# Skip product of a state-space layer folded into the addition of its outputs on VectorE

## The chip, the cores and the metric

The program runs on one core of one Trainium2 chip. The metric is the device time of one execution in microseconds (us); the time before is a median of three runs. One execution was also recorded by the hardware profiler, and every row of a trace below comes from that one.

## What is computed

The reference is one layer: a state-space mixer (Mamba-2 style, 16 sequences of 512 tokens, model width 128, inner width 256 in 4 heads), a layer norm, a mixture of 8 experts with 2 per token, and a second layer norm. The part that the change is about is the last term of the scan's output:

```
def step(h, inp):
    dA_t, dt_t, x_t, B_t, C_t = inp
    dBx = (dt_t[:, :, None] * x_t)[..., None] * B_t[:, None, None, :]
    h = dA_t[:, :, None, None] * h + dBx
    y = jnp.einsum('bn,bhpn->bhp', C_t, h) + D[None, :, None] * x_t
    return (h, y)
...
yn = y * jax.lax.rsqrt(jnp.mean(y * y, axis=-1, keepdims=True) + EPS) * norm_w
y = yn * jax.nn.silu(z)
return y @ Wout.T
...
x = _layernorm(x + _L0_attn_ref(x, ...), axis=-1)
x = _layernorm(x + _L0_ffn_ref(x, ...), axis=-1)
```

`D[None, :, None] * x_t` is the skip product: the activated channels of x, each times one number of its head.

## The kernel before, in words

Everything is written out by hand for each engine, with semaphores between the engines; each engine takes its instructions strictly in the order of the program. There is no scheduler.

**Stages.** A prologue turns the inputs of all sequences and starts sequence 0. Then come 16 slots, one for each sequence. Slot s does three things at once: it scans sequence s (`scan`), it projects and convolves sequence s + 1 (`project`), and it normalises and routes sequence s - 1 (`route`). After the slots, 135 tiles of 128 sorted rows go through the experts, and the last sums and norms close the program. Slot 0 has no sequence to route but finishes the softplus of all others (lines 1345 to 1347); slot 15 has nothing to project.

**A slot.** A slot goes over four chunks of 128 tokens, c = 0 to 3. For each chunk:
- TensorE (`slot_pe`) turns x and B (lines 652, 654), takes the outer products of C with the state for c > 0 (L658), projects a block of the next sequence (L483), adds up the chunk's output in PSUM bank `p7` (L676, L682), and makes the new state in `p6` (L691).
- VectorE (`slot_dve`) makes `Xdt` (L1313), `carried` (L1319), the mask `M` of the following chunk (L1107) and three taps of the convolution (L1033) of the next sequence; then the output `yv` (L1335), which is `p7` plus the skip product `xD`; then the new state (L1340 for c = 0, L1343 after it). In chunk 0 the layer-norm statistics of the routed sequence (L1140, L1144, L1147) stand between `Xdt` and `M`.
- ScalarE (`slot_act`) copies B (`Btok`, L907), takes exponentials (L773), the convolution's first tap (L815) and the squares of the outputs (`square`, L868, of `yv` into `ysq`).
- GpSimd multiplies `yv` by the gate (`gate_y`, L1547) and decays states, and scatters rows.

After chunk 3 TensorE computes the first gate block (L491), the sums of squares (L712, which waits for all four squares), the output product (L720), the inner products of the next sequence (L580) and the second gate block (L491 again). ScalarE then loads the table for Silu and goes through `activate` (L821, four of 128x512 into `xc`), `skip_part` (L826, two of 128x512 from `xc` into `xD`, with a scale per channel) and `gate_part` (L832, two into `sz`). VectorE ends the slot with the taps of block 3, the gates and top-2 of the routed sequence, `ms` (L1371) and the residual (`residual`, L1131).

**Waits around the change.** `yv` waits for the chunk's sum in PSUM (`y_psum`), for `xD_ready`, for the square of the chunk before (`sq_done`) and for the gate product of the chunk before (`g_ready`), since there are two `yv` buffers. The lines are

```
dve.wait_ge(y_psum, n + 1)
dve.wait_ge(xD_ready, CC * (s.n + 1))
wait(dve, sq_done, n - 1)
wait(dve, g_ready, n - 1)
dve.tensor_tensor(yv[c % 2][:, :, :], p7[:, 0:DI].rearrange("p (k d) -> p k d", k=CC),
                  xD[s.par][:, :, c * P:(c + 1) * P], ALU.add).then_inc(yv_ready, 1)
```

`xc`, `sz` and `xD` have two buffers each, taken by turns over the sequences. In the prologue `xD[1]` is also the landing place of two input sequences (`land`).

Of the kernel before, what the change touches and what calls it, by code (L numbers as in the profile page):

```python
# [24 lines left out]
ACT = mybir.ActivationFunctionType  # L25
AX_X = mybir.AxisListType.X

P = 128
SEQS, TOKS = 16, 512
NC = TOKS // P  # L30
H, HD = 4, 64
DI = H * HD
CC = DI // P
XC = CC + 2
# [47 lines left out]
def wait(eng, sem, value):  # L82

    if not isinstance(value, int) or value > 0:
        eng.wait_ge(sem, value)


def build(nc, t, out):
    ctx = ExitStack()
    with ctx:  # L90
        def sb(name, shape, dt=F32):
            return ctx.enter_context(nc.sbuf_tensor(name, shape, dt))

        def bank(name):
            return ctx.enter_context(nc.psum_tensor(name, [P, 512], F32))

        def sem(name):
            return ctx.enter_context(nc.semaphore(name))
# [14 lines left out]
        skip = sb("skip", [P, CC])  # L113
# [27 lines left out]
        acc = sb("acc", [P, XC, TOKS])  # L141
        xc = [sb(f"xc{i}", [P, XC, TOKS]) for i in range(2)]
        sz = [sb(f"sz{i}", [P, CC, TOKS]) for i in range(2)]
        xD = [sb(f"xD{i}", [P, CC, TOKS]) for i in range(2)]
        vals = sb("vals", [P, SEQS, 5, NC * H])
        cur = [sb(f"cur{i}", [P, 5, NC * H]) for i in range(2)]
        parts = sb("parts", [P, SEQS, KS], BF16)
# [18 lines left out]
        yv = [sb(f"yv{i}", [P, CC, P]) for i in range(2)]  # L166
        ysq = sb("ysq", [P, CC, TOKS])
        gt = sb("gt", [P, CC, TOKS])
# [52 lines left out]

        land = ([Gm[:, :, :], uT[:, :].rearrange("p (c d) -> p c d", c=NC)]
                + [big[:, k, :].rearrange("p (c d) -> p c d", c=NC)
                   for big in (xc[1], sz[1], xD[1], ysq, gt) for k in range(2)]
                + [xc[1][:, k, :].rearrange("p (c d) -> p c d", c=NC) for k in range(2, 4)]
                + [rowB[0][:, :, 0:P], rowB[1][:, :, 0:P]])

# [35 lines left out]
        p7 = bank("p7")  # L263
        h_bank = (pl[0], pl[1], p5)

        def y_bank(j):
# [16 lines left out]
        (xT_psum, dt_psum, proj_psum, z_psum, sums_psum, diff_psum, G_psum, tr_psum, off_psum, y_psum,  # L283
         state_psum, ss_psum, out_psum, uT_psum, logit_psum, rank_psum, S_psum) = [sem(n) for n in names_pe]
        names_act = ("xT_ready", "abs_done", "ev_ready", "L_ready", "tap0_done", "Btok_ready", "sq_done", "cur_ready", "S_ready",
                     "uT_ready", "rowB_ready", "eg_ready", "decays_ready", "xc_ready", "sz_ready",
                     "xD_ready")
        (xT_ready, abs_done, ev_ready, L_ready, tap0_done, Btok_ready, sq_done, cur_ready, S_ready, uT_ready, rowB_ready,
         eg_ready, decays_ready, xc_ready, sz_ready, xD_ready) = [sem(n) for n in names_act]
        names_dve = ("x1_ready", "Gm_ready", "M_ready", "Xdt_ready", "v_ready", "yv_ready", "state_ready",  # L290
                     "sp_step", "a_ready", "tap_done", "conv_done", "carried_ready", "ln_step", "ve_ready", "shift_ready",
                     "u_ready", "gate_step", "chosen_ready", "ms_ready", "pos_step", "rank_read",
# [468 lines left out]
        def _(act):  # L761
# [13 lines left out]
            def enter_x(q):  # L775
                act.wait_ge(xT_psum, q + 1)
                act.copy(xT[:, q, :], (p5, p7)[q % 2][:, :]).then_inc(xT_ready, 1)

            def enter_dt(g, lo, hi):

                w = (hi - lo) * NC * H
                act.wait_ge(v_ready, g + 1)
                act.activation(ev[:, 0:w], v[:, 0:w], ACT.Abs).then_inc(abs_done, 1)
                act.wait_ge(abs_done, g + 1)
                act.activation(ev[:, 0:w], ev[:, 0:w], ACT.Exp, scale=-1.0).then_inc(ev_ready, 1)
# [26 lines left out]
            def tap0(q, c):  # L812
                act.wait_ge(proj_psum, XC * q.n + c + 1)
                wait(act, xc_ready, XC * (q.n - 1) + c + 1)
                act.activation(acc[:, c, :], pj[c % 2][:, :], ACT.Identity, bias=conv_b[:, c:c + 1],  # L815
                               scale=conv_w[:, c, TAPS - 1:TAPS]).then_inc(tap0_done, 1)

            def activate(q, k):
                act.wait_ge(conv_done, XC * q.n + k + 1)
                wait(act, y_psum, NC * (q.n - 1))  # L820
                act.activation(xc[q.par][:, k, :], acc[:, k, :], ACT.Silu).then_inc(xc_ready, 1)  # L821

            def skip_part(q, k):
                act.wait_ge(xc_ready, XC * q.n + k + 1)
                wait(act, yv_ready, NC * (q.n - 1))
                act.activation(xD[q.par][:, k, :], xc[q.par][:, k, :], ACT.Identity,  # L826
                               scale=skip[:, k:k + 1]).then_inc(xD_ready, 1)

            def gate_part(q, k):
                act.wait_ge(z_psum, CC * q.n + k + 1)  # L830
# [3 lines left out]
            def enter_all():  # L834
                q = Seq(0, 0)
                enter_x(0)
                enter_x(1)
                act.wait_ge(w_early, 16 * W_EARLY)
                tap0(q, 0)
                enter_dt(0, 0, G0)  # L840
                tap0(q, 1)
                for k in range(2, 6):
                    enter_x(k)
                decay(1, 0, G0, 2, 5)
                tap0(q, 2)
                enter_x(6)
                enter_x(7)
                keep_parts(q, p6[0:KS, P:2 * P])
                tap0(q, 3)
                enter_x(8)  # L850
                enter_x(9)
                exp_exponents(0, 0)
                set_current(q)
                for k in range(10, 12):
                    enter_x(k)
                act.wait_ge(w_in, 16 * W_LOADS)
                for k in range(XC):
                    activate(q, k)
                    enter_x(12 + k)
                for k in range(CC):  # L860
                    skip_part(q, k)
                for k in range(CC):
                    gate_part(q, k)

# [30 lines left out]
            def slot_act(s, scan, project, route):  # L895
                q, r = s.plus(1), s.plus(-1)
                if project and not scan:
                    enter_all()
                    return
                for c in range(NC):  # L900
                    n = NC * s.n + c
                    if scan and c > 0 and (c + 1 < NC or project):
                        exp_exponents(n + 1, c + 1)
                    if scan and c + 1 < NC:
                        act.wait_ge(tr_psum, n + 1)
                        wait(act, state_psum, (NC - 1) * s.n + c - 1)
                        act.copy(Btok[c % 2][:, :], p5[:, CC * P:(CC + 1) * P]).then_inc(Btok_ready, 1)  # L907
                    if scan and c == 0:
                        exp_exponents(n + 1, c + 1)
                    if not route and c == 0:  # L910
                        enter_dt(1, G0, SEQS)
                    if s.n == 1 and c == 0:
                        decay(3, G0, SEQS, 4, 5)
                    if project and c == 1:
                        keep_parts(q, p4[0:KS, 0:P])
                    if route and c == 1:
                        for k in range(NC):
                            normalise(r, k)
                    if project:
                        tap0(q, c)  # L920
                    if project and c == 3:
                        set_current(q)
                    if scan and c > 0:
                        square(s, c - 1)
                    if route and c == 1:
                        keep_turned(r)
                    if route and c == 2:
                        second_rows(r)
                        exp_logits(r)
                if scan:  # L930
                    square(s, NC - 1)
                if not route:
                    decay(2, G0, SEQS, 2, 4)
                if project:
                    for k in range(XC):
                        activate(q, k)
                    for k in range(CC):
                        skip_part(q, k)
                    for k in range(CC):
                        gate_part(q, k)  # L940

            slots(act, slot_act)


# [25 lines left out]
            for j in range(TILES):  # L970
# [8 lines left out]
                n, step = divmod(j - FIN_AT - 8, FIN_TILES)  # L979
# [15 lines left out]
        def _(dve):  # L995
# [282 lines left out]
            def slot_dve(s, scan, project, route):  # L1278
                q, r = s.plus(1), s.plus(-1)
# [23 lines left out]
                for c in range(NC):  # L1303
                    n = NC * s.n + c
# [24 lines left out]
                        tap(q, c - 1, 3)  # L1329
                    if scan:  # L1330
                        dve.wait_ge(y_psum, n + 1)
                        dve.wait_ge(xD_ready, CC * (s.n + 1))
                        wait(dve, sq_done, n - 1)
                        wait(dve, g_ready, n - 1)
                        dve.tensor_tensor(yv[c % 2][:, :, :], p7[:, 0:DI].rearrange("p (k d) -> p k d", k=CC),  # L1335
                                          xD[s.par][:, :, c * P:(c + 1) * P], ALU.add).then_inc(yv_ready, 1)
                    if scan and c + 1 < NC:
                        dve.wait_ge(state_psum, (NC - 1) * s.n + c + 1)
                        if c == 0:
# [43 lines left out]
                if not project:  # L1383
                    fetch(2)
                    fetch(3)

            slots(dve, slot_dve)

            def add_rows(n):
# [32 lines left out]
            for j in range(TILES):  # L1422
# [31 lines left out]
                n, step = divmod(j - FIN_AT, FIN_TILES)  # L1454
# [20 lines left out]
            n = SEQS - 1  # L1475
# [254 lines left out]
```

## Time and profile before

| | us |
|---|---|
| Time, median of 3 runs | 731.25 |
| Lowest and highest run | 729.77, 731.27 |
| The profiled execution, own time | 729.96 |
| The profiled execution, span of the trace | 728.2 |
| Mean granted TensorE clock, as a share of full speed | 0.976 |

The span runs from the first to the last recorded instruction; 1.8 us of the execution's own time lie around it. In the span the prologue takes the first 38 us, the 16 slots run to about 430, and the expert tiles with the ending fill the rest. A slot in the middle takes about 24.1 us.

How to read the rows: times are microseconds from the start of the span unless marked ns. PE is TensorE, PEld its loading of weights, DVE is VectorE, ACT is ScalarE, POOL is GpSimd. L1335 is line 1335 of the kernel. `[0.57 <-ACT Btok L907]` says that the engine had stood idle for 0.57 us before this instruction, until ScalarE's instruction of line 907 released it.

### The profile page before, as it was taken

Reading aid. Unit: us, or ns where it says so; the run is one execution under the profiler, and the core shown is the slowest. Engines: PE = TensorE matmul, PEld = TensorE weight load, DVE = VectorE, ACT = ScalarE, POOL = GpSimd, SP = SyncE. Lnnn points to the kernel's source line nnn. Section 1 sums busy time; section 2 is a strip of 40 time slices with the busy share of each in tenths; the row PEclk is TensorE's granted clock in tenths of the full one; section 3 lists DMA queues with packets and bytes.
Section 4 is the critical chain, followed back from the end, with each engine's and each line's share of the span. In section 5 each row is a group of like instructions: output and inputs, shape, how many; then the busy total and the mean of one; then the engine's idle time right before and its main releaser. Section 6 shows DMA issues by size and latency. Waiting matters only on the chain.

```text
span 728.2 us, 19939 instructions
## 1 busy us (share of the span) xinstructions
PE 656.8 (90%) x5075; PEld 539.5 (74%) x5075; DVE 567.1 (78%) x1876; ACT 472.8 (65%) x1174; POOL 459.5 (63%) x664
## 2 busy tenths in 40 slices
PE   7978999999999999999999679999999999999910
PEld 5846756676666666756675569999999999999910
DVE  3478898999899999999999857677666666888744
ACT  3746767776777676767676527765656656677724
POOL 5022367777777776777677565767775455677754
PEclk9999999999999999999999999999999999999975
DMA  9180001101110111011101022332432223455443
GB/s 254 38 289 15 2 26 35 45 20 42 30 45 20 42 32 43 23 39 34 41 24 37 16 74 56 91 86 79 101 94 71 75 72 94 140 164 171 140 173 123
DMA packets 56543, 54.54 MB, mean 75 GB/s; under 512 B 9562, under 2 KB 45790, under 8 KB 56176
## 3 DMA queue, kind: packets, MB, share of 16 engines
q1 hardware_dynamic: 45712, 33.67, 16.9%
q0 software_dynamic: 8416, 16.93, 6.8%
q10 hardware_dynamic: 2304, 2.65, 1.0%
q8 instruction: 46, 0.75, 0.5%
q14 instruction: 65, 0.53, 0.3%
HBM read 31.05 MB, written 22.63 MB: 74 GB/s over the span
## 4 chain that ended last, share of the span: by engine, by line
PE 71%; DVE 9%; issue 8%; DMA 3%; POOL 3%; ACT 2%; SPq 1%; DVEq 1%; ACTq 0%; POOLq 0%
PE p L630 12%; PE pl L621 8%; PE pj L483 6%; PE p L682 4%; PE p L712 4%; PE p L621 4%; PE p L676 4%; PE p L720 3%; PE p L658 3%; PE p L691 2%; PE pj L491 2%; PE p L594 2%; PE p L580 2%; PE p L491 2%; PE pl L527 2%
## 5 line engine op out<-in xcount | busy, mean ns | idle before, releaser
L1651 POOL DMA_INDIRECT moe_rows<-xT x135 | 134.9, 999 | 79.6 <-DVE xT L1275 47.5
L1584 POOL DMA_INDIRECT sorted_rows<-pair,slot x128 | 128.6, 1004 | 32.5 <-issue 30.4
L1033 DVE SCALAR_TENSOR_TENSOR acc<-pj,conv_w_sb,acc 128x511 f32<-128x511 f32 (+2 forms) x192 | 142.3, 741 | 4.6 <-ACT acc L815 1.6
L630 PE MATMUL p<-w,xT 128*128 x1080 | 143.5, 276 | 1.6 <-ACT xT L950 1.3
L950 ACT ACTIVATE xT<-pl,b_sb 128x128 f32<-128x128 f32 x360 | 102.7, 369 | 47.5 <-PE pl L621 45.7
L630 PEld LDWEIGHTS p<-w,xT 128*128 128x128 f32 x1080 | 131.4, 192 | 2.8 <-issue 2.8
L621 PE MATMUL pl<-xT 128*128 128x128 f32 x720 | 95.1, 275 | 2.4 <-DVE xT L1263 2.4
L1271 DVE TENSOR_TENSOR xT<-p,b_sb 128x128 f32<-128x128 f32 x135 | 39.3, 291 | 64.5 <-PE p L630 60.6
L621 PEld LDWEIGHTS pl<-xT 128*128 128x128 f32 x720 | 87.5, 192 | 2.5 <-issue 2.5
L815 ACT ACTIVATE acc<-pj,conv_b_sb,conv_w_sb 128x512 f32<-128x512 f32 x64 | 49.5, 773 | 33.6 <-PE pj L483 33.6
L483 PE MATMUL pj<-xT,w_xbc 128*128 128x512 f32 x128 | 67.2, 607 | 0.0
L676 PEld LDWEIGHTS p<-M,Xdt 128*64 128x64 f32 x512 | 27.4, 136 | 53.4 <-issue 49.4
L950 ACT ACTIVATE xT<-p,b_sb 128x128 f32<-128x128 f32 x180 | 51.4, 370 | 23.7 <-PE p L621 23.4
L1597 POOL TENSOR_TENSOR Xdd<-Xdt,cur 128x256 f32<-128x256 f32 x48 | 29.5, 615 | 57.4 <-DVE Xdt L1313 49.0
L1263 DVE COPY xT<-w 128x512 f32 x135 | 58.5, 433 | 0.1
L1547 POOL TENSOR_TENSOR gt<-yv,sz 128x256 f32<-128x256 f32 x64 | 47.1, 736 | 11.4 <-DVE yv L1335 10.7
L1275 DVE SCALAR_TENSOR_TENSOR xT<-xT 128x128 f32<-128x128 f32 x135 | 48.7, 361 | 4.8
L676 PE MATMUL p<-M,Xdt 128*64 128x128 f32 x512 | 42.4, 285 | 10.4 <-issue 7.7
L773 ACT ACTIVATE pl<-pl 128x512 f32<-128x512 f32 x64 | 37.5, 586 | 16.5 <-PE pl L509 16.3
L621 PE MATMUL p<-xT 128*128 128x128 f32 x360 | 47.6, 275 | 0.0
L1107 DVE TENSOR_TENSOR M<-pl,Gm 128x512 f32<-128x512 f32 x64 | 43.8, 685 | 2.0 <-ACT pl L773 1.4
L621 PEld LDWEIGHTS p<-xT 128*128 128x128 f32 x360 | 43.8, 192 | 0.1
(223 smaller groups left out, 1406.8 us busy)
## 6 DMA issues: line engine op xcount, KB each, us to landing
xT<-sorted_rows SPq DMA_DIRECT2D x135, 65.0 KB, 2.4
xres<-in_x SPq DMA_DIRECT2D x16, 256.0 KB, 3.0
w<-in_w SPq DMA_DIRECT2D x2, 2048.0 KB, 10.0
acc<-moe_rows SPq DMA_DIRECT2D x12, 256.0 KB, 3.8
xT<-moe_rows SPq DMA_DIRECT2D x12, 256.0 KB, 5.5
out<-sz ACTq DMA_DIRECT2D x10, 256.0 KB, 2.6
moe_rows<-xT POOLq DMA_INDIRECT x135, 2.3
sorted_rows<-pair,slot POOLq DMA_INDIRECT x128, 2.4
```

The costliest lines, as they stand in the source:

```text
L483: pe.matmul(pj[k % 2][:, :], w_xbc[:, k * P:(k + 1) * P], xT[:, q.n, :], start=True, stop=True).then_inc(proj_psum, 1)
L621: mm = pe.matmul(h_bank[j % 3][:, f * P:(f + 1) * P], w1e[j % 4][:, f * P:(f + 1) * P], sT[j % 4], start=True, stop=True)
L630: mm = pe.matmul(y_bank(j)[:, 0:P], hT[j % 4][:, f, :], w2[:, bass.ds(e, 1), f, :].rearrange("p e d -> p (e d)"), start=(f == 0), stop=(f ...
L676: mm = pe.matmul(p7[half, (h // 2) * P:(h // 2 + 1) * P], Xdt[c % 2][:, h * HD:(h + 1) * HD], M[c % 2][:, h, :], start=(h < 2), stop=(c == ...
L815: act.activation(acc[:, c, :], pj[c % 2][:, :], ACT.Identity, bias=conv_b[:, c:c + 1], scale=conv_w[:, c, TAPS - 1:TAPS]).then_inc(tap0_do ...
L950: act.activation(hT[j % 4][:, f, :], h_bank[j % 3][:, f * P:(f + 1) * P], ACT.Gelu, bias=b1[:, bass.ds(e * FB + f, 1)]).then_inc(hT_ready, 1)
L1033: ins = dve.scalar_tensor_tensor(out=acc[:, k, j:TOKS], in0=pj[k % 2][:, 0:TOKS - j], scalar=conv_w[:, k, TAPS - 1 - j:TAPS - j], in1=acc[ ...
L1263: dve.tensor_copy(w1e[j % 4], w1[:, bass.ds(expert[j], 1), :].rearrange("p e f -> p (e f)")).then_inc(w1e_ready, 1)
L1275: dve.scalar_tensor_tensor(out=ye[j % 8], in0=ye[j % 8], scalar=xs[k][:, P + 1:P + 2], in1=xs[k][:, 0:P], op0=ALU.mult, op1=ALU.add).then_ ...
L1547: pool.tensor_tensor(gt[:, :, c * P:(c + 1) * P], yv[c % 2][:, :, :], sz[s.par][:, :, c * P:(c + 1) * P], ALU.mult).then_inc(g_ready, 1)
L1584: pool.indirect_dma_start(out=sorted_rows[:, :], out_offset=bass.IndirectOffsetOnAxis(slot[q.par][:, c, k:k + 1], 0), in_=(rowA, rowB)[k][ ...
L1651: pool.indirect_dma_start(out=moe_rows[:, :], out_offset=bass.IndirectOffsetOnAxis(xs[k][:, P:P + 1].bitcast(I32), 0), in_=ye[j % 8], in_o ...
```

## The change

ScalarE's two skip products of a sequence (`skip_part`), their tile `xD` and their semaphore `xD_ready` go. VectorE's one addition over 128x256 (`yv` = `p7` + `xD`) becomes two instructions over 128x128, one for each block k of channels: `xc` times the channel's number `skip[:, k]`, plus `p7`. Only the second of them raises `yv_ready`. The wait for `xD_ready` is dropped. ScalarE's `activate` waits, for k = 0 and 1, until the outputs of the sequence two before are done, since VectorE now reads `xc`; that condition stood in `skip_part` before. A tile `land_mem` of the size of one `xD` takes its place as a landing place of inputs.

```diff
-        xD = [sb(f"xD{i}", [P, CC, TOKS]) for i in range(2)]
+        land_mem = sb("land_mem", [P, CC, TOKS])
...
-                   for big in (xc[1], sz[1], xD[1], ysq, gt) for k in range(2)]
+                   for big in (xc[1], sz[1], land_mem, ysq, gt) for k in range(2)]
...
             def activate(q, k):
                 act.wait_ge(conv_done, XC * q.n + k + 1)
                 wait(act, y_psum, NC * (q.n - 1))
+                if k < CC:
+                    wait(act, yv_ready, NC * (q.n - 1))
                 act.activation(xc[q.par][:, k, :], acc[:, k, :], ACT.Silu).then_inc(xc_ready, 1)
-
-            def skip_part(q, k):
-                act.wait_ge(xc_ready, XC * q.n + k + 1)
-                wait(act, yv_ready, NC * (q.n - 1))
-                act.activation(xD[q.par][:, k, :], xc[q.par][:, k, :], ACT.Identity,
-                               scale=skip[:, k:k + 1]).then_inc(xD_ready, 1)
...
-                    for k in range(CC):
-                        skip_part(q, k)
                     for k in range(CC):
                         gate_part(q, k)
...
                         dve.wait_ge(y_psum, n + 1)
-                        dve.wait_ge(xD_ready, CC * (s.n + 1))
                         wait(dve, sq_done, n - 1)
                         wait(dve, g_ready, n - 1)
-                        dve.tensor_tensor(yv[c % 2][:, :, :], p7[:, 0:DI].rearrange("p (k d) -> p k d", k=CC),
-                                          xD[s.par][:, :, c * P:(c + 1) * P], ALU.add).then_inc(yv_ready, 1)
+                        for k in range(CC):
+                            ins = dve.scalar_tensor_tensor(
+                                out=yv[c % 2][:, k, :], in0=xc[s.par][:, k, c * P:(c + 1) * P],
+                                scalar=skip[:, k:k + 1], in1=p7[:, k * P:(k + 1) * P], op0=ALU.mult, op1=ALU.add)
+                        ins.then_inc(yv_ready, 1)
```

How VectorE's queue reads in chunk 0 of a slot that routes, around the output. Before:

```order
L1313 TENSOR_TENSOR Xdt<-p,cur 128x256 [waits Xdd_ready,Btok_ready,tr_psum]
L1140 BN_STATS st<-pair 128x6 [waits u_ready,x1_ready]
L1140 BN_STATS st<-pair 128x6 x3
L1144 BN_AGGR mv<-st 128x2 [waits ln_step,const_ready]
L1144 BN_AGGR mv<-st 128x2 x3
L1147 TENSOR_SCALAR ve<-mv 128x4 [waits ln_step]
L1107 TENSOR_TENSOR M<-pl,Gm 128x512 [waits y_psum,L_ready,Gm_ready]
L1335 TENSOR_TENSOR yv<-p,xD 128x256 [waits sq_done,g_ready,xD_ready,y_psum]
L1340 COPY state<-p 128x256 [waits state_psum]
```

With the change (its lines are numbered a few lower), the last rows of the same place:

```order
L1138 TENSOR_SCALAR ve<-mv 128x4 [waits ln_step]
L1098 TENSOR_TENSOR M<-pl,Gm 128x512 [waits y_psum,L_ready,Gm_ready]
L1326 SCALAR_TENSOR_TENSOR yv<-xc,skip,p 128x128 [waits g_ready,sq_done,y_psum]
L1326 SCALAR_TENSOR_TENSOR yv<-xc,skip,p 128x128
L1333 COPY state<-p 128x256 [waits state_psum]
```

The output is now two instructions with three waits in front of the first, in the same place: behind the mask of chunk 1 and ahead of the copy of the state. Nothing else on VectorE has another neighbour, and nothing on TensorE or GpSimd moves.

## Rows read from the trace of the kernel before

**Rows 1.** The page: span, and busy time of the engines.

```profile
span 728.2 us, 19939 instructions
PE 656.8 (90%) x5075; PEld 539.5 (74%) x5075; DVE 567.1 (78%) x1876; ACT 472.8 (65%) x1174; POOL 459.5 (63%) x664
```

**Rows 2.** Busy by stretch, slot 5: PE, PEld, DVE, ACT, POOL, clock, DMA, GB/s.

```profile
188.60:212.70 24.10, 22.98 (x168) 15.94 (x165) 21.95 (x68) 17.43 (x34) 17.80 (x29) 1.00 0.12 34
```

**Rows 3.** The chain that ended last, slot 5: start us, us, what.

```profile
189.78 0.27 ACT Btok L907
190.20 0.28 issue
...
192.64 0.15 DVE yv L1335
...
192.97 0.42 DVE state L1340
193.44 0.70 PE p L658 x2
...
206.15 0.99 PE pj L491 x2
207.14 2.00 PE p L712 x16
```

**Rows 4.** Waits of the slots (60 to 430 us), TensorE alone.

```profile
PE p L658 <- DVE state L1340: 5.7, 15, 0.4
```

**Rows 5.** Timeline, slot 5, VectorE.

```profile
195.05 0.46 DVE L1151 SCALAR_TENSOR_TENSOR shift<-mv,rstd 128x4 f32<-128x4 f32 x1
...
199.47 0.42 DVE L1313 TENSOR_TENSOR Xdt<-p,cur 128x256 f32<-128x256 f32 x1 [0.60 <-PE p L654]
...
202.84 0.74 DVE L1033 SCALAR_TENSOR_TENSOR acc<-pj,conv_w_sb,acc 128x511 f32<-128x511 f32 x1
203.66 0.42 DVE L1313 TENSOR_TENSOR Xdt<-p,cur 128x256 f32<-128x256 f32 x1
204.10 0.42 DVE L1319 TENSOR_TENSOR carried<-p,cur 128x256 f32<-128x256 f32 x1
...
206.19 0.42 DVE L1335 TENSOR_TENSOR yv<-p,xD 128x256 f32<-128x256 f32 x1 [0.23 <-ACT ysq L868]
...
211.20 1.12 DVE L1131 SCALAR_TENSOR_TENSOR pair<-p,rms,xres 128x128 f32<-128x128 f32 x4
```

**Rows 6.** Timeline, slot 5, ScalarE.

```profile
189.78 0.27 ACT L907 COPY Btok<-p 128x128 f32<-128x128 f32 x1 [0.52 <-PE p L654]
...
195.55 1.65 ACT L876 ACTIVATE pair<-pair,shift,rstd 128x128 f32<-128x128 f32 x4 [0.20 <-DVE shift L1151]
...
206.64 0.42 ACT L868 ACTIVATE ysq<-yv 128x256 f32<-128x256 f32 x1 [0.45 <-DVE yv L1335]
...
210.47 1.32 ACT L826 ACTIVATE xD<-xc,skip 128x512 f32<-128x512 f32 x2
211.69 0.57 ACT L832 ACTIVATE sz<-pj 128x512 f32<-128x512 f32 x1
```

**Rows 7.** Groups of instructions, shapes apart: busy us, mean ns, idle before.

```profile
L1271 DVE TENSOR_TENSOR xT<-p,b_sb 128x128 f32<-128x128 f32 x135 | 39.3, 291 | 64.5 <-PE p L630 60.6 <-issue 3.3
L1335 DVE TENSOR_TENSOR yv<-p,xD 128x256 f32<-128x256 f32 x64 | 26.7, 417 | 5.3 <-PE p L682 3.5 <-ACT ysq L868 1.8
L1131 DVE SCALAR_TENSOR_TENSOR pair<-p,rms,xres 128x128 f32<-128x128 f32 x64 | 18.0, 344 | 1.6 <-PE p L720 1.2 <-issue 0.3
L826 ACT ACTIVATE xD<-xc,skip 128x512 f32<-128x512 f32 x32 | 21.1, 707 | 0.0
```

**Rows 8.** Timeline, slots 0 and 15, where an output is covered or not.

```profile
50.22 0.42 DVE L1343 TENSOR_TENSOR state<-p,decayed 128x256 f32<-128x256 f32 x1 [0.40 <-PE p L691]
...
412.45 0.42 DVE L1340 COPY state<-p 128x256 f32<-128x256 f32 x1 [0.42 <-PE p L691]
...
427.04 2.02 PE L712 MATMUL p<-ones,ysq 128*128 128x96 f32 x16 [0.96 <-ACT ysq L868]
```

More of the change, by code:

```diff
@@ L285, in build @@
         names_act = ("xT_ready", "abs_done", "ev_ready", "L_ready", "tap0_done", "Btok_ready", "sq_done", "cur_ready", "S_ready",
-                     "uT_ready", "rowB_ready", "eg_ready", "decays_ready", "xc_ready", "sz_ready",
-                     "xD_ready")
+                     "uT_ready", "rowB_ready", "eg_ready", "decays_ready", "xc_ready", "sz_ready")
         (xT_ready, abs_done, ev_ready, L_ready, tap0_done, Btok_ready, sq_done, cur_ready, S_ready, uT_ready, rowB_ready,
-         eg_ready, decays_ready, xc_ready, sz_ready, xD_ready) = [sem(n) for n in names_act]
+         eg_ready, decays_ready, xc_ready, sz_ready) = [sem(n) for n in names_act]
         names_dve = ("x1_ready", "Gm_ready", "M_ready", "Xdt_ready", "v_ready", "yv_ready", "state_ready",
@@ L936, in slot_act @@
                         activate(q, k)
-                    for k in range(CC):
-                        skip_part(q, k)
                     for k in range(CC):
```

## Prediction
> **What bounds the kernel now.** I read the page first, for the engines' busy shares. TensorE is busy 90% of the span, VectorE 78%, ScalarE 65% [rows 1]. The change touches only the slots, so I then read the busy time by stretch. In a slot of 24.1 us TensorE is busy 22.98 us, VectorE 21.95 and ScalarE 17.43, at full TensorE clock [rows 2]. Two engines are nearly full there, so shares alone don't decide: what counts is at which places VectorE holds TensorE up. Those I took from the chain that ended last, laid over one slot, and then from the timelines of each engine in the same slot.
>
> The chain runs over TensorE for most of the slot and leaves it twice [rows 3]. The first time is at the start: ScalarE's copy Btok, VectorE's statistics, yv of chunk 0 at 192.64, the state at 192.97, and then TensorE's L658 at 193.44. TensorE had nothing to do for up to 0.4 us there, in 15 slots and for 5.7 us together [rows 4]. The second place is less plain. TensorE's gate block L491 starts at 206.15 and L712 follows at 207.14, 0.99 us later [rows 3], with no wait shown. But L712 waits for the last square, and that runs from 206.64 to 207.06, after 0.45 us of idling for yv of chunk 3 [rows 6]. So L712 starts 0.08 us after its square ends, and the square starts when yv has ended. Both places have a yv directly on the way to TensorE.
>
> **What goes.** ScalarE loses 32 instructions of 707 ns, 21.1 us in all [rows 7], 1.32 us per sequence [rows 6]. I cost this at nothing. Behind them stand the two gate parts. The first, at 211.69 [rows 6], will start about 1.2 us sooner; what needs it is TensorE's first block of the next slot, which stands behind the second gate block and the next exponents and transposes, and GpSimd's gating, later still. The second waits for TensorE's second gate block, so it does not move, and after it ScalarE idles 0.52 us for TensorE before Btok [rows 6]. ScalarE's slack grows where it had slack. The new condition in front of the activations of k = 0 and 1 asks for outputs of the sequence two before, finished a whole slot earlier: nothing. The dropped wait for xD_ready also gives nothing I can see, as xD is ready long before, and yv of chunk 3 starts in the same hundredth (206.19) in which its square ends [rows 5].
>
> **What comes.** One addition of 417 ns becomes two multiply-adds over 128 columns. No row shows a multiply-add whose second input is in PSUM and first in SBUF; the nearest is the residual L1131, over 128x128 with a scalar per partition, one input in PSUM, 344 ns each [rows 7]. Durations overlap: four of L1131 take 1.12 us [rows 5], so one starts (1.12 - 0.344) / 3 = 0.26 us after another. A pair then ends after 0.26 + 0.344 = 0.60 us, against 0.417: 0.19 us later. For the instruction behind it the price is the same: before, it starts 0.33 us after yv (192.64 to 192.97 [rows 3]); now, after 2 x 0.26 = 0.52. I take **0.19 us per chunk**. The lower end is a pair of plain additions over 128 columns, 291 ns [rows 7], that start 0.21 us apart (0.26 less the 0.05 that the scalar costs, 344 - 291): 0.21 + 0.291 - 0.417 = 0.08. The upper end is two of 344 that don't overlap: 0.27. A gain is excluded, since a second start comes on top of the same columns.
>
> The page "VectorE: DVE Perf Modes" of the Trainium skill speaks against such a split: its section on the TRN2 errata says that every instruction pays a fixed latency, so that small tiles pay it often, and gives (N + 151) / 0.96 ns for an fp32 addition of N columns. By that a pair costs an extra 151 / 0.96 = 157 ns, an estimate from the page; the rows agree with the formula (291 ns for 128 columns). The sum below would be 4.9 us by it instead of 5.9.
>
> **Which of the 64 lie on the path.** For the 14 slots 1 to 14, chunk by chunk:
> - Chunk 0: yes. The state's copy and L658 move by 0.19. VectorE has no gap from there to the shift at 195.05, and ScalarE's normalising at 195.55 waits for that shift [rows 5, 6]; all of it and TensorE move by the same 0.19, so nothing is added twice.
> - Chunk 1: no. VectorE idles 0.60 us before Xdt of chunk 2 [rows 5], and 0.19 fits.
> - Chunk 2: no, but barely. A tap starts at 202.84 and its successor could start about 0.65 us later, at 203.49 (my reading of the overlap); Xdt starts at 203.66, held by TensorE's transposes. Then carried starts at 204.10, 0.44 after Xdt instead of the usual 0.33 [rows 5]. That is 0.17 + 0.11 = 0.28 us of slack for 0.19.
> - Chunk 3: yes. yv starts when the square of chunk 2 lets it (a wait of 0.23 [rows 5]), its end moves by 0.19, and so do the last square and L712. The taps, gates and residual move along with TensorE, which has moved as much.
>
> That makes 28. In slot 0, VectorE's softplus work holds TensorE up; chunk 1 is covered by the state's wait of 0.40 us for TensorE [rows 8], and chunk 3 by TensorE's gate block; I count 2. In slot 15 chunk 0 is covered, as the state waits 0.42 us for TensorE, chunks 1 and 2 likewise, while L712 waits 0.96 us for the square of chunk 3 [rows 8]: 1. Together 31 x 0.19 = **5.9 us**. The experts' stage starts that much later and does the same work. The profiled execution takes 729.96 us, so 735.9 for it; it lies 1.3 us under the median of 731.25, by which I forecast **737.1 us**, 0.8% slower. A measurement of this kernel can tell about 0.2%, or 1.5 us, from no change.
>
> **The rivals.**
> - *The pair costs more.* The second multiply-add waits until the first has left the engine: 0.27 us per chunk, 31 x 0.27 = 8.4 us, 739.6. Chunk 2's slack of 0.28 would just hold. Against it, four L1131 overlap [rows 5]. The same page's section on the DRAIN says that an instruction starts only when the one before has left the pipe, with exceptions for inputs and outputs that start on the same partitions; the trace shows the exception. 0.14.
> - *All 64 count.* VectorE becomes the bound of a slot: 64 x 0.19 = 12.2 us, 743.4; at 0.27, 748.5. It decides if VectorE's gaps are gone. A slot has 24.10 - 21.95 = 2.15 us of them [rows 2], against 4 x 0.19 = 0.76. 0.04.
> - *Nothing to measure.* One of the two places is covered by something I don't see (TensorE's gate block before L712 leaves only about a tenth of a microsecond), and the pair costs its lower end: 17 x 0.08 = 1.4 us, 732.6. 0.08.
> - *Faster.* ScalarE's end of the slot is what starts the next one. The chain has Btok for 0.27 us and 0.28 us of issue behind it in each slot [rows 3]. If ScalarE came to Btok late because of the skip products in front, up to 0.55 us would go in each of 15 slots, 8.2 us, and with the 5.9 paid the time is 731.25 - 2.3 = 729.0. It decides if ScalarE is still busy when TensorE's transpose for Btok ends. Against it, ScalarE stands idle for 0.52 us just then [rows 6]. 0.04.
>
> The forecast itself (31 places, near 0.19) gets 0.70.
>
> **How the numbers follow.** The forecast's own spread is 29 to 33 places at 0.13 to 0.24 us, 3.8 to 7.9 us. The range of 8 in 10 reaches from 733.0, below which lie the faster case, the unmeasurable one and a pair near its lower end, to 741.0, above the costlier pair with a run's scatter; 743 and more is left out. Faster by over 0.2%: 0.04. Within 0.2%: the third rival and a sliver of the forecast, 0.08. Slower: the rest, 0.88.
>
> **What would show it.** The multiply-adds should have a mean near 344 ns, and a pair should end 0.60 us after its start. Slots should be 0.38 us longer, 24.1 to 24.5. TensorE's wait for the state should grow from 0.38 to about 0.57 us in slots 1 to 14, and L712 should start some 1.2 us after its gate block instead of 0.99. VectorE's gap before Xdt of chunk 2 should shrink to about 0.4 us. ScalarE should be busy 21 us less and idle that much more. The prediction fails if the pair takes under 0.5 us, if VectorE shows no gap left in a slot (then more than two chunks count), or if the last square moves and L712 does not.

## Result, and the profile after

| | before | after |
|---|---|---|
| Time, median of 5 runs each | 731.07 us | 734.66 us |
| Lowest and highest | 729.39, 731.27 | 734.15, 737.37 |
| The profiled execution, own time | 729.96 us | 737.37 us |
| Its span, mean granted clock | 728.2 us, 0.976 | 735.6 us, 0.973 |

The ratio of the times is 1.0069, with a 95% interval of 1.0056 to 1.0082: the change makes the kernel slower by 5.0 us (4.1 to 6.0). The medians of the table lie 3.6 us apart and the means of the same runs 4.8; I go by the ratio, and by the slots of the traces below, which are the finer measure. The profiled execution after is the longest of its five, so its 7.4 us over the profile before overstate the change; part of why is below. One correction to the labels ahead of the prediction: the slot that its rows show as slot 5 is, counted from 0, the slot s = 6. Nothing hangs on the number; I keep to that slot.

The page after, its span and the engines' busy times, and the busy time of the same slot (columns as in [rows 2]):

```profile
span 735.6 us, 19879 instructions
PE 658.6 (90%) x5075; PEld 540.6 (73%) x5075; DVE 578.2 (79%) x1940; ACT 453.3 (62%) x1142; POOL 460.1 (63%) x664
```

```profile
191.06:215.49 24.43, 22.97 (x163) 15.90 (x162) 22.57 (x72) 16.21 (x32) 17.77 (x29) 1.00 0.12 34
```

The slot has grown from 24.1 to 24.43 us; TensorE does the same work in it, VectorE 0.6 us more, ScalarE 1.2 us less. The groups of the new instructions (as in [rows 7]) and TensorE's waits from 60 to 430 us (as in [rows 4]):

```profile
L1326 DVE SCALAR_TENSOR_TENSOR yv<-xc,skip,p 128x128 f32<-128x128 f32 x128 | 38.3, 341 | 4.8 <-ACT ysq L861 1.8 <-PE p L681 1.7 <-POOL gt L1540 1.1
```

```profile
PE p L657 <- DVE state L1333: 8.2, 15, 0.6
...
PE p L711 <- ACT ysq L861: 1.8, 12, 0.2
```

The wait for the state of chunk 0 has gone from 5.7 to 8.2 us in the same 15 slots [rows 4], 0.17 us each. A second wait is new in the middle slots: TensorE's sums of squares stand behind the last square, 12 times for 0.15 us each. Before, the same list has this wait only once, 1.0 us in slot 15 (the 0.96 of [rows 8]), which in the changed kernel falls behind 430 us. TensorE at this place in the slot:

```profile
208.77 1.12 PE L490 MATMUL pj<-xT,w_z 128*128 128x512 f32 x2
210.05 2.02 PE L711 MATMUL p<-ones,ysq 128*128 128x96 f32 x16 [0.15 <-ACT ysq L861]
```

The sums start 1.28 us after the gate block; in the same view of the kernel before it is 207.11 - 206.01 = 1.10. VectorE's timeline in the slot:

```profile
195.22 0.59 DVE L1326 SCALAR_TENSOR_TENSOR yv<-xc,skip,p 128x128 f32<-128x128 f32 x2
195.73 0.41 DVE L1333 COPY state<-p 128x256 f32<-128x256 f32 x1
...
202.24 0.42 DVE L1304 TENSOR_TENSOR Xdt<-p,cur 128x256 f32<-128x256 f32 x1 [0.42 <-issue]
...
208.94 0.61 DVE L1326 SCALAR_TENSOR_TENSOR yv<-xc,skip,p 128x128 f32<-128x128 f32 x2 [0.23 <-ACT ysq L861]
```

The pair takes 0.59 to 0.61 us, and the state starts 0.51 us after it (0.33 before). The gap ahead of Xdt of chunk 2 is 0.42 us where it was 0.60 [rows 5]: chunk 1's growth has gone into it. ScalarE's end of the slot:

```profile
209.58 0.42 ACT L861 ACTIVATE ysq<-yv 128x256 f32<-128x256 f32 x1 [0.63 <-DVE yv L1326]
210.02 1.28 ACT L822 ACT_TABLE_LOAD   x1
211.31 2.19 ACT L822 ACTIVATE xc<-acc 128x512 f32<-128x512 f32 x4
213.41 0.58 ACT L827 ACTIVATE sz<-pj 128x512 f32<-128x512 f32 x1
215.68 0.60 ACT L827 ACTIVATE sz<-p 128x512 f32<-128x512 f32 x1 [1.70 <-PE p L490]
```

The square waits 0.63 us for yv instead of 0.45 [rows 6], and the freed time of the skip products stands whole in front of the second gate part, as idling for TensorE: 1.70 us, where it was 0.48.

### The profile page after: what moved, and what is told of

It is laid out like the page before. It is cut to its first block, busy times and chain, and to the rows that moved or that the text cites. A ratio compares the mean times of both kernels' runs of the same rounds, so it can differ in the third digit from the quotient of the medians.

```text
span 735.6 us, 19879 instructions
## 1 busy us (share of the span) xinstructions
PE 658.6 (90%) x5075; PEld 540.6 (73%) x5075; DVE 578.2 (79%) x1940; ACT 453.3 (62%) x1142; POOL 460.1 (63%) x664
## 4 chain that ended last, share of the span: by engine, by line
PE 60%; POOL 11%; issue 10%; DVE 10%; ACT 3%; DMA 3%; SPq 1%; DVEq 1%; POOLq 0%; ACTq 0%
PE p L629 12%; PE pl L620 8%; PE pj L482 4%; PE p L620 4%; PE p L711 4%; PE p L719 3%; POOL moe_rows L1644 3%; POOL sorted_rows L1577 2%; PE p L657 2%; PE p L675 2%; PE p L681 2%; DVE yv L1326 2%; PE p L579 2%; PE p L490 2%; PE pl L526 2%
## 5 line engine op out<-in xcount | busy, mean ns | idle before, releaser
L620 PE MATMUL pl<-xT 128*128 128x128 f32 x720 | 96.6, 278 | 2.6 <-DVE xT L1254 2.6
```

Of the source, the lines that this page charges most:

```text
L620: mm = pe.matmul(h_bank[j % 3][:, f * P:(f + 1) * P], w1e[j % 4][:, f * P:(f + 1) * P], sT[j % 4], start=True, stop=True)
```

## The experiments

The time of a whole run scatters by a few us (the kernel before took 726.98 to 731.76 in the 29 runs beside e1 to e4), but the slots in the middle of a profiled execution agree within some hundredths, so I read both: the ratio to runs of the kernel before that were taken together with it, and the mean period of four slots in the middle (from the start of the sums of squares in slot 6 to that in slot 10, by 4). The kernel before gives (303.38 - 207.11) / 4 = 24.07 us, the changed one (307.80 - 210.05) / 4 = 24.44.

| run | edit | period, us | ratio of times (95%) |
|---|---|---|---|
| before | | 24.07 | 1 |
| change | | 24.44 | 1.0069 (1.0056 to 1.0082) |
| e1 | multiply-adds in chunks 1, 2 | 24.07 | 1.0009 (0.9995 to 1.0023) |
| e2 | plain split, xD kept | 24.19 | 1.0030 (1.0014 to 1.0045) |
| e3 | skip products gone, one addition | 24.07 | 0.9999 (0.9987 to 1.0011) |
| e4 | change, last square apart | 24.37 | 1.0057 (1.0036 to 1.0077) |
| e5 | multiply-adds in chunk 0 | 24.27 | 1.0035 (1.0020 to 1.0050) |
| e6 | multiply-adds in chunk 3 | 24.26 | 1.0038 (1.0023 to 1.0053) |
| e7 | e4, Silu chain early | 24.31 | 1.0059 (1.0039 to 1.0080) |
| e8 | change, state first | 24.60 | 1.0114 (1.0093 to 1.0136) |
| e9 | before, rows early | 23.67 | 0.9914 (0.9883 to 0.9945) |
| e10 | change, rows early | 24.20 | 1.0013 (0.9997 to 1.0030) |
| e11 | e9, last square apart | 23.64 | 0.9883 (0.9858 to 0.9907) |

**Where the price falls: e1, e5, e6.** ScalarE's skip products are kept in all three, and only the output of some chunks is made by multiply-adds (e1 is shown; e5 has `c == 0` and e6 `c == 3`). ScalarE's `activate` waits for the outputs of the sequence two before, as in the change:

```diff
+                        if c in (1, 2):
+                            for k in range(CC):
+                                ins = dve.scalar_tensor_tensor(...)
+                            ins.then_inc(yv_ready, 1)
+                        else:
                             dve.tensor_tensor(yv[c % 2][:, :, :], ...
```

> The two multiply-adds in chunks 1 and 2 only; chunks 0 and 3 add xD as before, and ScalarE still makes xD. Theory (only chunks 0 and 3 have no cover): a slot in the middle stays at 24.07 us, the last slot's sums of squares start near 427 as before (slot 0 may give 0.4 us), the time is within 0.2% of before. Rival (VectorE's load as a whole sets the slot): half of the change's growth, 0.18 us per slot, 24.25 us, about 3 us slower.

Measured: 24.07 us, and a ratio that holds 1. Chunks 1 and 2 cost nothing, and VectorE's load as such is not what sets the slot. In e1's timeline of VectorE the pair of chunk 1 and what it runs into:

```profile
196.52 0.59 DVE L1339 SCALAR_TENSOR_TENSOR yv<-xc,skip,p 128x128 f32<-128x128 f32 x2
197.03 0.41 DVE L1352 TENSOR_TENSOR state<-p,decayed 128x256 f32<-128x256 f32 x1
197.36 0.74 DVE L1035 SCALAR_TENSOR_TENSOR acc<-pj,conv_w_sb,acc 128x511 f32<-128x511 f32 x1
198.52 0.42 DVE L1315 TENSOR_TENSOR Xdt<-p,cur 128x256 f32<-128x256 f32 x1 [0.42 <-issue]
```

> The two multiply-adds in chunk 0 only; the rest adds xD, and ScalarE still makes it. Theory (chunk 0 costs its full price in every slot): slots of 24.07 + 0.18 = 24.25 us, the wait of TensorE for the state of chunk 0 grows from 0.39 to 0.57 us, the time 2.5 to 3 us above before. Rival (the whole price sits in chunk 3): 24.07 us, no difference.

> The two multiply-adds in chunk 3 only. Theory: slots of 24.07 + 0.18 = 24.25 us, the sums of squares start 0.15 us after the gate block has let go, the time 2.5 to 3 us above before. With chunk 0 alone and chunks 1 and 2 alone this should add up to the change's 0.37 us per slot. Rival (the two places hide one another, so each alone costs all of it or nothing): 24.07 or 24.43 us.

Measured: 24.27 and 24.26 us, 0.20 and 0.19 more than before; together 0.39, and the change has 0.37. The two places add up, so neither hides the other, and each alone costs about what I gave it. In times it is 0.35% and 0.38%, against 0.69% for the change. TensorE's waits in e5 and then in e6, from 60 to 430 us:

```profile
PE p L658 <- DVE state L1349: 8.2, 14, 0.6
```

```profile
PE p L658 <- DVE state L1349: 5.8, 15, 0.4
...
PE p L712 <- ACT ysq L870: 1.9, 12, 0.2
```

Each has one of the two longer waits of the changed kernel, and not the other.

**What the price is made of: e2.** The addition is split and nothing else:

```diff
-                        dve.tensor_tensor(yv[c % 2][:, :, :], p7[:, 0:DI]..., xD[...], ALU.add).then_inc(yv_ready, 1)
+                        for k in range(CC):
+                            ins = dve.tensor_tensor(yv[c % 2][:, k, :], p7[:, k * P:(k + 1) * P],
+                                                    xD[s.par][:, k, c * P:(c + 1) * P], ALU.add)
+                        ins.then_inc(yv_ready, 1)
```

> The addition of yv and xD is only split into two plain additions over 128x128, with no scalar; xD and ScalarE's work stay. Theory (the price is that of a second instruction): a plain addition of 128 columns takes 291 ns and the next can start about 0.21 us later, so a pair ends 0.50 us after its start against 0.417, 0.08 to 0.09 us per chunk, slots of 24.07 + 0.17 = 24.24 us, 2.5 to 3 us slower. Rival (the fixed cost per instruction of 0.157 us counts in full): 24.38 us, 4.9 us slower. Rival (the scalar operand alone is what costs): no difference to before.

Measured: 24.19 us, 0.12 more than before, where I expected 0.17, and 2.2 us in the time (1.0 to 3.3). The group and one pair with its successor:

```profile
L1336 DVE TENSOR_TENSOR yv<-p,xD 128x128 f32<-128x128 f32 x128 | 30.8, 282 | 5.5 <-PE p L682 4.7 <-ACT ysq L868 0.7
```

```profile
192.23 0.48 DVE L1336 TENSOR_TENSOR yv<-p,xD 128x128 f32<-128x128 f32 x2
192.63 0.41 DVE L1342 COPY state<-p 128x256 f32<-128x256 f32 x1
```

A plain addition took 282 ns, less than the 291 of [rows 7], and a pair ends after 0.48 us, 0.06 to 0.07 later than one of double width. The multiply-adds take 341 ns and end 0.18 to 0.19 later. So a third of the price is the second instruction, and two thirds are the scalar operand, 0.06 us in each of two instructions. The formula of the Trainium skill ("VectorE: DVE Perf Modes", the section on the TRN2 errata) comes to 291 ns for 128 columns, as in [rows 7] and 9 ns over the 282 of e2. Read as a price it puts 0.157 us on a split; that rival (24.38 us) is out, since neighbours overlap.

**What the gain is worth: e3.** ScalarE's skip products are gone as in the change, and VectorE's one addition reads `xc` where it read `xD`. The factor D is left out of the computation, so the work is the change's gain without its price.

> ScalarE's skip products go, and VectorE's one addition over 128x256 reads xc in place of xD: the factor D of the skip term is left out of the computation. It is the change's gain alone. Theory (ScalarE had slack at the slot's end): slots of 24.07 us, the time within 0.2% of before. Rival (ScalarE's relief is worth something, and the multiply-adds cost more than I say): slots shorter than 24.0 us, faster by over 0.2%.

Measured: 24.07 us and a ratio of 0.9999 with an interval from 0.9987 to 1.0011. ScalarE's 21 us are worth nothing here.

**How chunk 3 holds TensorE: e4 and e7.** In e4 the products of the first three chunks' squares don't wait for the fourth:

```diff
-                    pe.wait_ge(sq_done, NC * (s.n + 1))
+                    pe.wait_ge(sq_done, NC * (s.n + 1) - 1)
                     pe.wait_ge(yv_ready, NC * (s.n + 1))
                     for c in range(NC):
+                        if c == NC - 1:
+                            pe.wait_ge(sq_done, NC * (s.n + 1))
```

> The changed kernel, and TensorE waits for the last square only ahead of the products of chunk 3's squares, not ahead of all sixteen. Theory (yv of chunk 3 holds TensorE through the last square): the sums of squares start straight behind the gate block, so each slot is about 0.15 us of wait plus what was hidden in front of it (0.3 us in all) shorter, 24.43 to about 24.12 us, and the time is some 4.5 us less than the change's, near before. Rival (the last square is no bound, TensorE's gate block is late by itself, or the residual and ms hold the slot's end): 24.43 us, no difference to the change.

Measured: 24.37 us. The first half of the theory came true and the second did not: TensorE starts the sums 0.32 us sooner, and the slot is only 0.07 us shorter than the changed kernel's. Its timeline in the slot, and below it ScalarE's:

```profile
207.19 1.12 PE L490 MATMUL pj<-xT,w_z 128*128 128x512 f32 x2
208.15 1.96 PE L713 MATMUL p<-ones,ysq 128*128 128x96 f32 x16
209.94 1.98 PE L721 MATMUL p<-w_out,gt 128*128 128x128 f32 x16
211.97 1.16 PE L579 MATMUL p<-xc 128*128 128x128 f32 x8
```

```profile
208.43 1.28 ACT L824 ACT_TABLE_LOAD   x1
209.72 2.19 ACT L824 ACTIVATE xc<-acc 128x512 f32<-128x512 f32 x4
```

L713 follows 0.96 us behind L490 instead of 1.28. But L721 runs from 209.94 for 1.81 us (the distance of its successor in the changed kernel), and L579 comes only at 211.97, 0.06 us after ScalarE's last activation ends at 211.91. Behind the last square stands a second way to TensorE: load of the table, four activations, inner products. It had 0.2 us of slack and becomes the bound at once. e7 takes that away too:

```diff
                 if scan and c > 0:
                     square(s, c - 1)
...
+                if project:
+                    activate(q, 0)
                 if scan:
                     square(s, NC - 1)
...
-                    for k in range(XC):
+                    for k in range(1, XC):
                         activate(q, k)
```

> The kernel of e4 (changed kernel, last square waited for apart), and ScalarE's first activation of the next sequence, with the load of its table, stands ahead of the last square instead of behind it. In e4 TensorE's inner products started 0.06 us after ScalarE's last activation had ended, so I think that yv of chunk 3 holds TensorE twice: through the last square and through the Silu chain behind that square. Theory: with both freed, slots lose 0.3 us against the change, 24.43 to about 24.11 us, and the time lies some 4.5 us under the change's. Rival (e4's small gain has another cause, the residual or ms for instance): 24.37 us as in e4.

Measured: 24.31 us, between theory and rival. The inner products are freed, but my own edit puts the last square behind the table's load and one activation. It now starts 1.85 us after its `yv` (182.99 to 184.84) instead of 0.64 (208.94 to 209.58 in the changed kernel), so 1.2 us later, and TensorE's last products wait for it. These rows are from the end of the slot before:

```profile
183.78 2.21 PE L713 MATMUL p<-ones,ysq 128*128 128x96 f32 x16
185.82 1.98 PE L721 MATMUL p<-w_out,gt 128*128 128x128 f32 x16
187.63 1.06 PE L579 MATMUL p<-xc 128*128 128x128 f32 x8
```

L721 to L579 takes 1.81 us again, but L713 to L721 takes 2.04 where it took 1.86. Of 0.32 us gained at the start of the sums 0.18 are paid back there, and 0.14 are left; the slot is 24.44 - 24.31 = 0.13 us shorter. I count the two ways out of the last square as shown: the sums moved when they were freed in e4, and the inner products when they were freed on top of that in e7. The Silu chain was never freed alone, and that the slot would reach 24.11 us with both free was not shown.

**How chunk 0 holds TensorE: e8.** The copy of the state goes ahead of yv:

```diff
+                    if scan and c == 0:
+                        dve.wait_ge(state_psum, (NC - 1) * s.n + c + 1)
+                        dve.tensor_copy(state[0][:, :], p6[:, DI:2 * DI]).then_inc(state_ready, 1)
                     if scan:
                         dve.wait_ge(y_psum, n + 1)
...
-                        if c == 0:
-                            dve.tensor_copy(state[0][:, :], p6[:, DI:2 * DI]).then_inc(state_ready, 1)
```

> The changed kernel, and in chunk 0 VectorE copies the state ahead of yv. Theory A (only the state's copy holds TensorE at that place): L657 starts 0.5 us sooner and slots shrink by as much, 24.43 to about 23.9 us. Theory B (the whole of VectorE's queue up to the shift holds TensorE there, by ScalarE's normalising and the turning of rows): TensorE waits less for the state and more for the rows, and slots stay at 24.43 us. I hold B for likelier.

Measured: 24.60 us, slower than either said. VectorE and then TensorE in e8:

```profile
194.68 0.69 DVE L1098 TENSOR_TENSOR M<-pl,Gm 128x512 f32<-128x512 f32 x1
195.42 0.42 DVE L1323 COPY state<-p 128x256 f32<-128x256 f32 x1
195.76 0.59 DVE L1329 SCALAR_TENSOR_TENSOR yv<-xc,skip,p 128x128 f32<-128x128 f32 x2
...
198.06 0.47 DVE L1142 SCALAR_TENSOR_TENSOR shift<-mv,rstd 128x4 f32<-128x4 f32 x1
```

```profile
195.90 0.70 PE L657 MATMUL p<-state,xc 128*128 128x256 f32 x2 [0.19 <-DVE state L1323]
...
197.91 0.66 PE L675 MATMUL p<-M,Xdt 128*64 128x128 f32 x8 [0.40 <-issue]
...
200.30 0.63 PE L587 MATMUL p<-ident,pair 128*128 128x128 f32 x4 [0.66 <-issue]
```

TensorE gets the state 0.39 us sooner (its wait is 0.19 instead of 0.58) and gives it up again at two later waits, for Xdt of chunk 1 (0.40, where the changed kernel has none) and for the rows (0.66, where it has 0.58). So B holds in its mechanism, not in its number: what bounds this part, in this order of the work, is VectorE's queue from Xdt to the shift. The slot is 0.16 us longer, and 0.13 of that is a gap on this queue: the state's copy starts 0.74 us after the mask, where a successor follows after 0.60 to 0.61, as TensorE's product for it (L690, 194.73 to 195.38) had only just ended.

**A faster kernel, and what the change costs in it: e9, e10, e11.** If the queue up to the shift is the bound, the shift should not stand behind work that nobody waits for. On the kernel before:

```diff
+                    if route and c == 0:
+                        shift_rows(r)
                     if c == 0 and s.n >= 2:
                         take_ranks(s.plus(-2))
...
-                    if project and c > 0:
+                    if project and c > 0 and not (route and c == 1):
                         tap(q, c - 1, 1)
...
-                    if route and c == 1:
-                        shift_rows(r)
+                    if project and route and c == 1:
+                        tap(q, c - 1, 1)
                     if scan and c + 1 < NC:
                         mask_chunk(s, c + 1)
```

and on ScalarE the four `normalise` stand ahead of `keep_parts` in chunk 1.

> The kernel before, with the layer norm's shift on VectorE straight behind the state of chunk 0 (ahead of the ranks, a tap, Xdt and carried), the first tap of block 0 behind carried, and ScalarE's normalising ahead of its copy of the split sums. Theory (from e8: VectorE's queue from Xdt of chunk 0 to the shift holds TensorE at the turning of rows, for 0.58 us): the turning of rows starts straight behind L691, slots of 24.07 - 0.58 = 23.5 us, some 8 us faster than before. Rival (another wait takes its place, the copy of the split sums or Xdt of chunk 1): less than 0.2 us per slot gained.

Measured: 23.67 us per slot and 0.86% less time (0.55 to 1.17%), faster than both kernels; the period gains 0.40, not 0.58. Everything that was measured together with e9 to e11 took longer: the kernel before had 773.33 us there and 730.14 beside e1 to e4. It had no profile of its own there, but the three traces show where the time lies: from the last sums of squares to the end of the span e9 takes 342 us, e10 343 and e11 342, against 301 in the kernel before, while parts of a slot that no edit touches are as long as ever (6.55 us from the sums of squares to the next slot's first L483 in e9 and in the kernel before). So only ratios are compared; why the stage is longer stays open. TensorE in e9:

```profile
192.72 0.60 PE L691 MATMUL p<-Xdd,Btok 128*128 128x256 f32 x2
193.16 0.60 PE L588 MATMUL p<-ident,pair 128*128 128x128 f32 x4
```

The rows are turned straight behind L691, and the 0.58 us of idling are gone. The missing 0.18 lies at two places in the timelines. From L658 of chunk 1 to L588 TensorE gains even 0.75 us (3.11 instead of 3.86). It gives back 0.27 in chunk 2 (3.34 instead of 3.07 from L654 to L594) and 0.11 in chunk 0, where L676 starts 1.23 us after L483 instead of 1.12: from 60 to 430 us it waits 12 times for Xdt, 3.2 us in all, and before once, 1.0 us. So the rival was right in part: other waits took some of the place.

> The same move on top of the changed kernel. Theory: yv of chunk 0 still holds the state and TensorE's L657, and yv of chunk 3 the last square, so the change costs its 0.37 us per slot here as well: 23.87 us, a time between before's and 3 us under it. Rival (with the rows early, VectorE's queue of chunk 0 has cover and only chunk 3 counts): 23.68 us.

Measured: 24.20 us, a ratio of 1.0013 (0.9997 to 1.0030): all that the move had won is lost again. The change costs 24.20 - 23.67 = 0.53 us per slot here, not 0.37. That is three chunks of 0.18. VectorE and TensorE in e9, and below them in e10:

```profile
193.82 0.41 DVE L1335 TENSOR_TENSOR yv<-p,xD 128x256 f32<-128x256 f32 x1
194.15 0.41 DVE L1343 TENSOR_TENSOR state<-p,decayed 128x256 f32<-128x256 f32 x1
...
195.31 0.42 DVE L1313 TENSOR_TENSOR Xdt<-p,cur 128x256 f32<-128x256 f32 x1
```

```profile
194.48 0.27 PE L654 MATMUL p<-ident,xc 128*128 128x128 f32 x1
194.62 0.70 PE L658 MATMUL p<-state,xc 128*128 128x256 f32 x2
```

```profile
197.62 0.59 DVE L1326 SCALAR_TENSOR_TENSOR yv<-xc,skip,p 128x128 f32<-128x128 f32 x2
198.14 0.42 DVE L1336 TENSOR_TENSOR state<-p,decayed 128x256 f32<-128x256 f32 x1
```

```profile
198.28 0.27 PE L653 MATMUL p<-ident,xc 128*128 128x128 f32 x1
198.61 0.70 PE L657 MATMUL p<-state,xc 128*128 128x256 f32 x2
```

With the rows early, the 0.60 us of VectorE's gap ahead of Xdt of chunk 2 are gone. In e9 the state of chunk 1 ends at 194.56, just as TensorE comes to it (L658 0.14 us behind L654); in e10 L657 comes 0.33 us behind L653, 0.05 after the state's end at 198.56. Chunk 1 has lost its cover. Both theories had chunk 1 covered, so both fell. That it is chunk 1 I read from these timelines; no run has the multiply-adds in chunk 1 alone in this order.

> e9 with the last square waited for apart. Theory: the sums of squares start straight behind the gate block and slots lose another 0.1 us, 23.4 us; the Silu chain was 0.2 us from holding TensorE and should just not. Rival: the Silu chain takes the square's place at once, as e9's 23.5 us.

Measured: 23.64 us, 0.9883 (0.9858 to 0.9907). The rival holds in the slot: 0.03 us against e9. L580 starts at 207.18, 0.05 us after ScalarE's last activation has ended (204.94 + 2.19), as in e4. The interval of the time overlaps e9's; I take the two as equal. Both beat the kernel before and the changed one.

## Why the prediction held

- *What it costs per chunk.* Forecast 0.19 us, measured 0.18 to 0.19: a pair of 0.59 to 0.61 us against 0.417, successors after 0.51 us instead of 0.33. The nearest row, L1131 [rows 7], had 344 ns; the new instructions have 341, so its second input in PSUM makes no difference.
- *Which chunks count.* 0 and 3 in slots 1 to 14, and they add up (e1, e5, e6). The slots grew by 0.37 us, forecast 0.38. The start of the last sums of squares moved from 427.04 to 433.33, by 6.3 us; 31 places gave 5.9. The 0.4 more lie at the ends: 0.61 us by slot 0's sums instead of 0.38, and 0.41 in slot 15 instead of 0.19. Slot 15 took 26.98 us before, 26.11 in e1 and 28.28 in e2, which no price of a pair explains, so I read nothing into 0.2 us there.
- *Chunk 2.* Its 0.28 us of slack for 0.19 held in e1. In the slot of the changed kernel Xdt of chunk 3 now follows the tap after 0.66 us (0.82 before), with carried 0.40 after it (0.44 before); it was as close as forecast.
- *The last square.* Right as a place, but told too simply. I had the square holding L712 alone; the Silu chain behind the same square holds the inner products almost as tightly (e4). The price was the same since both move together.
- *Chunk 0.* I named the state's copy and the queue to the shift together. e8 shows that the second is the bound in this order; the copy alone, moved ahead, gained nothing.
- *The gain.* Forecast nothing, measured nothing (e3).
- *The time.* Forecast 737.1 us, measured 734.66, within the range. As a difference it was 5.9 us forecast and 5.0 by the ratio, whose interval (4.1 to 6.0) just takes in 5.9. So the mechanism and the places are shown by the slots, and no term of the sum is shown to be over-sized. The step from slots to the whole, "the experts' stage starts that much later and does the same work", would be the one to suspect, but the profiled executions don't show it: their slots lost 6.3 us, and what comes after them took 302.3 us instead of 301.2, 0.9 of that by the clock (below).

## What to carry to other kernels

Taking work from an engine with slack and giving a smaller amount to one that stands right ahead of the bound costs the smaller amount, at each place where the receiver has no gap; the relief counts for nothing. Cover is a property of the present order: the same edit cost two chunks per slot here and three once a better order had used up a gap, so measure it again after each reordering. Where freeing one wait gives back most of its gain, look for a second way from the same instruction (here one square with two followers) before calling the first unimportant.

## What I had not expected of the hardware

TensorE's granted clock falls to half after some idle stretches and not after others that are as long. In slot 0 TensorE idles 2.35 or 2.36 us for Xdt of chunk 1. In the kernel before, the changed one, e3 and e6 its next products run at half clock (0.50 from 48 to 50 us in the first two), and L682 takes 1.22 or 1.23 us. In e1 the same idling is followed by 0.71, and so it is in seven more runs; e8 idles 3.00 us there and keeps its full clock. TensorE's timeline in the kernel before, and then in e1:

```profile
47.23 0.95 PE L676 MATMUL p<-M,Xdt 128*64 128x128 f32 x8 [2.35 <-issue]
48.11 1.22 PE L682 MATMUL p<-ident,carried 128*128 128x128 f32 x4
```

```profile
46.03 0.66 PE L676 MATMUL p<-M,Xdt 128*64 128x128 f32 x8 [2.35 <-issue]
46.62 0.71 PE L682 MATMUL p<-ident,carried 128*128 128x128 f32 x4
```

It happens again where the experts' stage begins. After 2.58 us of idling in the changed kernel, and 2.58 in e6:

```profile
440.20 2.04 PE L620 MATMUL pl<-xT 128*128 128x128 f32 x8 [2.58 <-DVE xT L1254]
```

```profile
436.92 1.13 PE L621 MATMUL pl<-xT 128*128 128x128 f32 x8 [2.58 <-DVE xT L1265]
```

That fall costs 0.9 us, and it is in the profiled execution after but not in the one before, so 0.9 of their 7.4 us are this. It doesn't come with the multiply-adds as such: e8 has them in all four chunks, idles 2.56 us there and keeps its full clock. In e1 and e11 the clock fell in this stage too, with no idling right ahead: in e1 the products after 433.43 take 1.65 us instead of 1.06. The five runs after fit: the two longest (737.37, 736.20) have a mean granted clock of 0.973, the three others (734.15 to 734.66) 0.977 to 0.978. What tells one idle stretch from the other these traces don't show.
